# A perceiver kernel: keys of the second layer projected one block earlier, the maxima of a block dealt to other tiles, unread products in TensorE's waits, and the silu in two halves

## What is computed

```
def layer0(x):
    h = layernorm(x)
    q, k, v = h @ Wq.T + bq, ctx @ Wk.T + bk, ctx @ Wv.T + bv      # 16 heads of 16
    x = x + softmax(q @ k.T / 4 + (1 - mask) * -10000) @ v          # mask: 128 x 12544
    x = x + causal_linear_attention(layernorm(x))                   # then a gelu feed-forward
    h = layernorm(x)                                                # inputs and weights quantized
    return x + bitlinear(silu(bitlinear(h, w_gate)) * bitlinear(h, w_up), w_down)   # 256 -> 1024 -> 256

def layer1(x):                                                      # weights of its own, no mask
    x = x + (softmax(q @ k.T / 4) @ v) @ Wo.T + bo
    x = x + rwkv_time_mix(layernorm(x))
    return x + conv_ffn(layernorm(x))
```

## Time and profile before

| | |
|---|---|
| time of three runs | 1090.59, 1091.87, 1091.94 us; median 1091.87 |
| profiled execution | 1094.2 us, its span 1092.5 us, mean granted clock 0.975 |
| busy, us of the span | PE 1024.6, DVE 743.1, ACT 679.3, POOL 420.0 |
| L1091 of block 7's seven tiles and of block 8's first | 246.89, 251.47, 256.57, 261.14, 265.73, 270.32, 275.78, 280.63 us |
| durations at full clock elsewhere in the trace | a unit of keys (L1042) 1.67, the turns (L1119) 0.66, eight products such as L1312's (L1365) 1.05 us |
| scores of block 14's tiles 0 and 1 | start at 592.00 and 597.41 us, 5.41 apart |
| DVE's waits in the pair stage | 2.06 us ahead of 573.70, 1.76 ahead of 587.73 |
| first layer's blocks, last layer's | some 38 to 512 us, 592 to 1049 us |

### The profile page before, as it was taken

One profiled execution on the slowest core, in us unless ns is written; L12 is line 12 of the kernel. 1 busy time (PEld: TensorE's weight loads), 2 busy tenths in 40 slices (PEclk: granted clock), 3 DMA queues, 4 the chain that ended last, 5 costly groups with the idle time before them and its releaser, 6 DMA issues. The chain is left out here.

```text
span 1092.5 us, 30637 instructions
## 1 busy us (share of the span) xinstructions
PE 1024.6 (94%) x12851; PEld 687.2 (63%) x12851; DVE 743.1 (68%) x1714; ACT 679.3 (62%) x951; POOL 420.0 (38%) x374
## 2 busy tenths in 40 slices
PE   7899999999999999977878899999999999999877
PEld 4466666666666666655544576666666666666655
DVE  4788888888888888766347756655656555556555
ACT  3677777777778787765542555555655556555632
POOL 4268888888888888760100000000000000000000
PEclk9899999999999999998987999999999999999998
DMA  7410122201222012130031010111100111000000
GB/s 305 137 59 29 52 69 69 69 19 52 69 70 69 19 53 69 52 133 22 10 134 49 2 32 6 35 36 36 35 15 22 36 35 36 2 2 2 2 1 6
DMA packets 14682, 53.31 MB, mean 49 GB/s; under 512 B 3025, under 2 KB 4817, under 8 KB 13649
## 3 DMA queue, kind: packets, MB, share of 16 engines
q1 hardware_dynamic: 14544, 51.35, 13.6%
HBM read 51.21 MB, written 0.13 MB: 47 GB/s over the span
## 5 line engine op out<-in xcount | busy, mean ns | idle before, releaser
L740 DVE TENSOR_REDUCE tile_max<-ps_max 128x1 f32<-128x448 f32 x416 | 241.9, 620 | 161.1 <-PE ps_max L1054 159.7
L737 DVE CUSTOM_DVE_ANT_0 unread<-ps_max,masks 128x448 bf16<-128x448 f32 x432 | 253.5, 621 | 70.6 <-PE ps_max L1054 68.5
L413 POOL TENSOR_TENSOR probs<-probs,masks 128x512 f32<-128x512 f32 x182 | 227.8, 1273 | 77.9 <-ACT probs L526 76.9
L533 ACT ACTIVATE probs<-probs 128x1024 f32<-128x1024 f32 x196 | 207.4, 1058 | 58.7 <-DVE probs L795 46.7
L538 ACT ACTIVATE probs<-ps_scores 128x1024 f32<-128x1024 f32 x193 | 187.2, 1021 | 90.4 <-PE ps_scores L1095 90.3
L1095 PE MATMUL ps_scores<-q_pad,k_full 32*128 32x256 f32 x3088 | 233.9, 380 | 0.0
L1111 PE MATMUL ps_out<-probs,values 128*32 128x128 f32 x6272 | 214.9, 278 | 6.0 <-ACT probs L533 4.9
L1111 PEld LDWEIGHTS ps_out<-probs,values 128*32 128x32 f32 x6272 | 161.4, 111 | 58.8 <-issue 50.1
L1054 PE MATMUL ps_max<-k_high,q_high 32*128 32x448 bf16 x848 | 183.7, 360 | 14.0 <-DVE tile_max L740 7.6
L1095 PEld LDWEIGHTS ps_scores<-q_pad,k_full 32*128 32x128 f32 x3088 | 193.8, 188 | 1.0
L1042 PE MATMUL ps_proj<-ctx_t,wk 128*128 128x448 f32 x368 | 163.4, 567 | 0.0
(11 more groups left out here) (249 smaller groups left out, 787.7 us busy)
## 6 DMA issues: line engine op xcount, KB each, us to landing
ctx_t<-in_ctx_t SPq DMA_DIRECT2D x28, 896.0 KB, 5.3
masks<-in_mask_n SPq DMA_DIRECT2D x14, 448.0 KB, 3.4
masks<-in_mask_t SPq DMA_DIRECT2D x14, 448.0 KB, 3.6
room_w<-in_L_attn_f_w SPq DMA_DIRECT2D x2, 1024.0 KB, 8.9
room_w<-in_L_ffn_w SPq DMA_DIRECT2D x2, 1024.0 KB, 7.5
room_w<-in_L_ffn_w_gate SPq DMA_DIRECT2D x1, 1024.0 KB, 10.4
room_w<-in_L_ffn_w_up SPq DMA_DIRECT2D x1, 1024.0 KB, 12.9
room_w<-in_L_ffn_w_down SPq DMA_DIRECT2D x1, 1024.0 KB, 14.9
```

Source lines behind the costliest of these rows:

```text
L413: nc.gpsimd.tensor_tensor(p, p, three(mask_t[m % 2], TILES)[:, t, :].unsqueeze(1).to_broadcast([P, 4, P]), ALU.add).then_inc(sig("bias_add ...
L533: nc.scalar.activation(prob(T, half), prob(T, half), ACT.Exp).then_inc(sig(f"exp_done{half}"), 1)
L737: ins = v.tensor_tensor_reduce(unread[:, j % 2, :], max_bank(m, j)[:, 0:HALF], mask_n[m % 2][:, HALF * half:HALF * (half + 1)], 1.0, -3e38 ...
L740: ins = v.tensor_reduce(tile_max[:, h, half:half + 1], ps_max[:, j % 2, 0:HALF], AX_X, ALU.max)
```

## The change

1. `EXTRA_AT` of the first layer goes from (0, 2, 3, 4) to (1, 3, 5, 6); at 6 the extra is one of the block after next. The second layer keeps (0, 2, 3, 4). Block 0 has its own deal, and changes at tile 6 alone.
2. The keys of block 14 are projected in block 12, at tiles 0, 2, 4 and 6. `BETWEEN` has 14 units in another order, `BESIDE` two (behind pairs 1 and 4, both read by ACT at pair 5).
3. Unread products: `idents` (128 columns) at the very start and after the first turn, and in block 13, ahead of and behind the quantized stage's transposes, in the pair stage (one behind each pair from 6 to 15, four ahead of L1125) products of 256 columns.
4. The silu's table is loaded by a product of one column right after `ln_root(4)`; the silu and the multiply behind it go in two halves of 512 columns.

```diff
-        EXTRA_AT = (0, 2, 3, 4)
+        EXTRA_AT = ((1, 3, 5, 6), (0, 2, 3, 4))
...
+            one = int(t in EXTRA_AT[m // NB])
             if n + 1 < NB:
-                if t < LAST_AT:
-                    now = (2 if n == 0 else int(t in EXTRA_AT), 2, 2)
-                elif t == LAST_AT:
-                    now = (0, 2, 0)
+                if n == 0:
+                    now = (2, 2, 2) if t < LAST_AT else (0, 2, 0) if t == LAST_AT else now
+                elif t <= LAST_AT:
+                    now = (one, 2, 2 if t < LAST_AT else 0)
             if n + 2 < NB:
-                ahead = (0, 0, 2) if t == LAST_AT else (0, 2, 2) if t > LAST_AT else (0, 0, 0)
+                ahead = (0, 0, 2) if t == LAST_AT else (one, 2, 2) if t > LAST_AT else ahead
...
-        BETWEEN = [("k", NB, j) for j in range(4)] + [("k", NB + 1, j) for j in range(4)]
-        BETWEEN += [("v", NB, u) for u in range(PAIRS)] + [("k", NB + 2, j) for j in range(3)]
-        BESIDE = [("k", NB + 2, 3)] + [("v", NB + 1, u) for u in range(PAIRS)]
-        BESIDE_AT = (1, 4, 7, 10, 13)
+        BETWEEN = [("k", NB + 1, 0), ("k", NB + 1, 1), ("v", NB, 0), ("v", NB, 1), ("k", NB + 1, 2), ("v", NB, 2), ("k", NB + 1, 3),
+                   ("k", NB + 2, 0), ("v", NB, 3), ("v", NB + 1, 0), ("v", NB + 1, 1), ("v", NB + 1, 2)]
+        BETWEEN += [("k", NB + 2, 1), ("k", NB + 2, 2)]
+        BESIDE = [("k", NB + 2, 3), ("v", NB + 1, 3)]
+        BESIDE_AT = (1, 4)
         def keys_in_block(m):
-            return m < BLOCKS and m not in (NB, NB + 1, NB + 2)
+            return m < BLOCKS and m not in (NB + 1, NB + 2)
...
                     ln_root(4)
+                    act.wait_ge(sig("table_loaded"), 2)
+                    nc.scalar.activation(stat[:, 30:31], ones[:, 0:1], ACT.Silu).then_inc(sig("table_loaded"), 1)
                     between_out(8, 9)
...
-                    act.wait_ge(sig("gate_ready"), 1)
-                    nc.scalar.activation(gelu, ps_scores[:, 0:2, :].rearrange("p a n -> p (a n)"), ACT.Silu,
-                                         scale=stat[:, 20:21]).then_inc(sig("silu_ready"), 1)
+                    for half in range(2):
+                        act.wait_ge(sig("gate_ready"), half + 1)
+                        nc.scalar.activation(gelu[:, 512 * half:512 * (half + 1)], ps_scores[:, half, :], ACT.Silu,
+                                             scale=stat[:, 20:21]).then_inc(sig("silu_ready"), 1)
...
+                    for half in range(2):
+                        cols = slice(512 * half, 512 * (half + 1))
+                        dve.wait_ge(sig("gate_ready"), 3 + half)
+                        dve.wait_ge(sig("silu_ready"), 1 + half)
+                        note(v.scalar_tensor_tensor(out=big[:, cols], in0=ps_scores[:, 2 + half, :], scalar=stat[:, 21:22],
+                                                    in1=gelu[:, cols], op0=ALU.mult, op1=ALU.mult))
...
+            def idents(n):
+                for _ in range(n):
+                    mm(ps_out[:, 0:P], ident[:, :], ident[:, :], start=True, stop=True)
 
             pe.wait_ge(sig("idents"), 3)
+            idents(4)
...
                         if i in BESIDE_AT:
                             beside_in(BESIDE_AT.index(i))
-                    for u in range(len(BESIDE)):
-                        beside_read(u)
+                        elif i > 5:
+                            idle_products(1, ps_out)
+                        if i == 5:
+                            for u in range(len(BESIDE)):
+                                beside_read(u)
                 read_by[0] = ("max_copied", NB * l + 1)
+                idle_products(2 + 2 * l, ps_proj)
                 turn_max(NB * l)
...
                         projections(m, t)
+                        if m == NB - 1 and t > SUMS_AT:
+                            proj_free(None)
+                            idle_products(1, ps_proj)
...
+                if l == 0:
+                    idle_products(3, ps_proj)
                 weigh(NB * l + NB - 1, TILES - 1)
```

More of the change, by code:

```diff
@@ L562, in _ @@
                 if l == 1:
-                    between_out(14)
+                    between_out(13)
                 turned(4 * l, ps_max[:, 0, 0:D], xn_t[:, :, :].rearrange("p c t -> p (c t)"))
@@ L639, in _ @@
                     nc.scalar.copy(bigt.bitcast(BF16)[:, 0:D], ps_max[:, 0, :].bitcast(BF16)[:, 0:D]).then_inc(sig("xq_ready"), 1)
-                    act.wait_ge(sig("gate_ready"), 1)
-                    nc.scalar.activation(gelu, ps_scores[:, 0:2, :].rearrange("p a n -> p (a n)"), ACT.Silu,
-                                         scale=stat[:, 20:21]).then_inc(sig("silu_ready"), 1)
-                    between_out(10, 11, 12, 13)
+                    for half in range(2):
+                        act.wait_ge(sig("gate_ready"), half + 1)
+                        nc.scalar.activation(gelu[:, 512 * half:512 * (half + 1)], ps_scores[:, half, :], ACT.Silu,
+                                             scale=stat[:, 20:21]).then_inc(sig("silu_ready"), 1)
+                    between_out(10, 11, 12)
                     act.wait_ge(sig("hq_turned"), 1)
@@ L912, in _ @@
                     out_(quant(xn[:, :], D, bigq.bitcast(BF16)[:, 0:D], (0, 1), 20), "xq_made")
-                    dve.wait_ge(sig("gate_ready"), 1)
-                    dve.wait_ge(sig("silu_ready"), 1)
-                    link(v.scalar_tensor_tensor(out=big, in0=ps_scores[:, 2:4, :].rearrange("p a n -> p (a n)"), scalar=stat[:, 21:22],
-                                                in1=gelu, op0=ALU.mult, op1=ALU.mult))
+                    for half in range(2):
[4 more added lines that the diff above has]
+                                                    in1=gelu[:, cols], op0=ALU.mult, op1=ALU.mult))
+                    dve.wait_ge(sig("dve_link"), links[0])
                     out_(quant(big, FF, bigq.bitcast(BF16), (2,), 22), "hq_made")
@@ L1175, in between_in, with idle_products @@
                     (keys_in if what == "k" else values_in)(m, j, between_bank(u))
-            def idle_products(n):
+            def idle_products(n, bank=ps_out):
                 for _ in range(n):
-                    mm(ps_out[:, 0:D], ident[:, :], wq[0][:, 0, :], start=True, stop=True)
+                    mm(bank[:, 0:D], ident[:, :], wq[0][:, 0, :], start=True, stop=True)
+            def idents(n):
+                for _ in range(n):
+                    mm(ps_out[:, 0:P], ident[:, :], ident[:, :], start=True, stop=True)
             pe.wait_ge(sig("idents"), 3)
+            idents(4)
             for l in range(2):
@@ L1185, in _ @@
                 turn(xn, ps_max[:, 0, :]).then_inc(sig("turned"), 1)
+                if l == 0:
+                    idents(1)
                 pe.wait_ge(sig(f"q_weights{l}"), 32)
@@ L1192, in _ @@
                 if l == 1:
-                    between_read(14)
+                    between_read(13)
                 for zz in range(2):
@@ L1303, in _ @@
                                           tern[n][:, FF * k + 512 * half:FF * k + 512 * (half + 1)], start=(k == 0), stop=(k == DC - 1))
-                    last.then_inc(sig("gate_ready"), 1)
-                    between_in(10, 11, 12, 13)
+                            last.then_inc(sig("gate_ready"), 1)
+                    between_in(10, 11, 12)
+                    idle_products(1, ps_proj)
                     pe.wait_ge(sig("hq_made"), 1)
@@ L1309, in _ @@
                     last.then_inc(sig("hq_turned"), 1)
+                    idle_products(2, ps_proj)
                     pe.wait_ge(sig("hq_ready"), 1)
@@ L1314, in _ @@
                     last.then_inc(sig("down_ready"), 1)
-                    between_in(14)
+                    between_in(13)
             idle_products(3)
```

## The result

The changed kernel takes 1103.79 us (median of 8 runs, 1097.85 to 1107.55), the kernel before 1092.47 (8 runs, 1090.59 to 1094.66): a ratio of 1.0101, 95% interval 1.0082 to 1.0121. It is 11 us slower, where 1091.3 and a chance of 0.31 for slower had been forecast. The profiled execution of after took 1104.66, its span is 1102.9. In all that follows, executions that were slowed as a whole (one each of f, i, j and q, in each the profiled one) are left out.

What follows compares the result with a forecast made beforehand. PE's program with short waits bounds steady blocks; elsewhere a PE, ACT and DVE chain and the lower clock do. Terms: 9.6 - 2.8 + 0.2 - 3.2 - 1.8 - 1.4 - 1.2 = -0.6, from 1091.87 to 1091.3; range 1085 to 1097.

Steps and rivals of the forecast that it cites:

- Part 1: First layer's extras moved to tiles 1, 3, 5, 6: +0.82 a steady block, +9.6 us in all.
- the prediction's upper bound: For the moved extras in blocks 1 to 11: +14 (11 x 1.27), if no key tile gains.
- Part 2: Block 14's keys projected in block 12 fill PE's waits behind the maxima: -2.8; tile 6's unit costs nothing.
- Part 3: Block 13, products behind each weigh: ring lengthened by 1.2, clock staying up saves 1.0; +0.2.
- Part 4: Between the layers: silu halves -1.6, last product at full clock -0.8, order of units -0.8; -3.2.
- Parts 5 and 6: Pair stage: one of DVE's two waits goes, -1.8. Block 14: one of two slow first tiles won back, -1.4.
- Part 7: Start: unread products bring full rate sooner, 0.7 from the first keys and 0.5 from small steps; -1.2.
- (b): First layer's extras cost nothing, biases of tiles 5 and 6 still starting on time: about 1077; chance 0.15.
- (d): Pair stage: unread products keep PE behind DVE, ten pairs of 0.6 more, +6: about 1097; chance 0.16.
- (c): Unread products keep the clock wherever they stand, blocks 14 and 0 starting at full clock: about 1087; chance 0.22.
- (e): No clock is won in block 13, between the layers, block 14 or the start: about 1095.7; chance 0.13.

Runs made afterwards that it cites:

- f: Run a's kernel without the fourteen unread products of the pair stage: 1085.80 us, ratio 0.9928 to the kernel before.
- i: Kernel before with only block 14's keys in block 12 and the new lists of units between and beside: 1088.61 us, ratio 0.9972.
- j: Run g's kernel with five more unread products around block 14's tiles 0 and 1: 1076.43 us, ratio 0.9885 to the kernel before.
- q: Run l's kernel with eight more unread products ahead of the turn of block 0's maximum: 1086.14 us, ratio 0.9938 to the kernel before.
- a: Changed kernel with the first layer's extras back at tiles 0, 2, 3, 4: 1088.24 us, ratio 0.9948 to the kernel before.
- c: Changed kernel with DVE adding the last block's sums ahead of tile 1's bias, blocks 1 to 12: 1094.13 us, ratio 1.0009 to the kernel before.
- b: Kernel before with only the first layer's extras moved to tiles 1, 3, 5, 6: 1104.01 us, ratio 1.0107.
- d: Kernel before with only the unread products of the start: 1090.07 us, ratio 0.9975.
- h: Kernel before with only the silu and the multiply in halves and the table loaded early: 1089.03 us, ratio 0.9968.
- l: Run c's kernel (sums added first) with the first layer's extras at tiles 1, 2, 3, 4: 1079.76 us, ratio 0.9887 to the kernel before.
- g: Run a's kernel with four more unread products in the waits of the second layer's queries: 1083.76 us, ratio 0.9914 to the kernel before.
- m: Run l's kernel with the nine unread products of g and j: 1078.85 us, ratio 0.9874 to the kernel before.
- n: Changed kernel with tile 6's extra maximum behind the keys' products instead of ahead of the bias: 1106.01 us, ratio 1.013 to the kernel before.
- p: Run l's kernel with four more unread products ahead of the turn of block 0's maximum: 1083.51 us, ratio 0.9904 to the kernel before.

## Why the prediction was wrong

The forecast was 12.5 too low, and the miss has two halves. The deal was to cost 9.6 and costs 15.6 (a against the changed kernel): 6.0 missed. Parts 2 to 7 were to give back 10.2 and give back some 3.5 (a against the kernel before): 6.7 missed, less if the interval of a is taken.

**Part 1, the step that failed: "its product takes PE 0.18, about half of it in a wait: +0.10".** Tile 1 was costed by the extra's product alone. I had written of tile 5 that the bias is later and asked who waits for it; of tile 1 I did not ask. There the sums (L786) stand behind the bias on DVE and the values behind the sums on PE. Before, the sums were over 0.30 ahead of the values; DVE now starts its first maximum of the tile 0.20 later and has one more (0.62) ahead of the bias, and 0.82 later they are not. Measured +0.57, so a steady block pays 1.27 and not 0.82, and blocks 1 to 12 5.6 more. Run c takes 0.46 of the 0.57 away by the order on DVE alone. The rest of part 1 held: tile 5 +0.75 (0.73), tile 6 +0.54 (0.54), tiles 0, 2 and 4 -0.20 each (-0.19). Tile 3 has its extra before and after the change, so its +0.01 is the price of nothing. That a block cost 1.27, the number of the prediction's upper bound, is chance: the bound had no tile 1 in it and let no key tile gain, and tile 1 lost 0.57 while the key tiles gained 0.60.

**Part 2** came near its number: block 12 is 2.1 shorter where 2.8 were forecast, with 0.47 lost at tile 1 and 0.33 at tile 6, which was held to be free. But the gain is not the time of the filled waits. Before, the three waits of 1.2 lie in tiles 0, 2 and 4, and these take 4.57 to 4.59, as in a steady block; long were tiles 1 and 5, 6.67 and 6.99 at the lower clock. Run b's block 12, without keys but at a clock of 1.00, takes 32.81, less than the 34.13 with them. What the keys seem to buy is the clock: none of the eight profiles with them has a low stretch in block 12, three of the four without them have one.

**Part 3** held. In all eight profiled kernels that have its products the last weigh takes 1.08 and the turns 0.66, in the four without them 1.60 to 1.94 and 1.08 to 1.09; from block 13's first scores to the end of the turns it is 29.58 for 29.63 (+0.2 forecast).

**Part 4** was right in the silu: the reduce starts 3.02 behind the gate's first matmul (561.48 - 558.46) where it was 4.52, and the two halves of the multiply take 1.41 in sum for 1.28, as its working had it. The last product takes 1.05, but it does so in b, d and h too, which have no unread products there: the 1.89 was that one execution's clock. The order of the units brought 0.1, not 0.8: from the end of the turns to the gate it is 34.54 for 34.64. Of 0.46 won by the first turn of x most is lost again at a multiply of DVE (L910), which takes 1.03 in every profile with the change and 0.42 in those without; why is not shown.

**Parts 5 and 6 are the other step that failed, and the sum itself was of the wrong kind.** "The first stays (its unit of keys stays), the second goes: -1.8" and "I take one of the two back: -1.4": I took each low stretch of one execution as the cost of a place, and crossed it off where products were put. The profiles show that the stretches lie elsewhere from one execution to the next. In after the pair stage lost 1.4 where 1.8 were to be won: DVE still waits twice, 2.77 and 2.10, as both units ran at the lower clock (3.36 and 3.78). Block 14's tile 0 was at full clock (3.96, before 5.41) and tiles 1 and 2 paid (6.39 and 5.47). With the same program of the pair stage its reduces take 21.64 from first to last in after, 19.11 in a and 17.15 in c and l. Filling one wait (g) did not end it in block 14; with the waits filled up to a place where PE is busy without a break (m) the one profile taken is free of it, and the times of j agree.

**Part 7** came to its number (-1.3 for -1.2) by other terms. The first keys take 1.74 and not 3.33, more than the 0.7 assumed, but they start 1.18 later (9.88 for 8.70). Block 0's own 2.3 in the profile of after had no part in the sum; it is the clock of that execution, since b has it without any product.

**The rivals.** (b), that the extras cost nothing, is refuted by run b. (d) named the pair stage as what would make it slower; it did cost there, but by its units at the lower clock, while behind pair 5 the pairs are 1.11 apart and not 1.65, and the +11 is not from it: with the pair products and the old deal the kernel is faster than before. (c) and (e) are tested by a, which lacks part 1's 9.6. (c) comes to 1087.3 - 9.6 = 1077.7 then; a's median is 1088.2, and one of its twelve runs reached 1078.23. (e), no clock is won, comes to 1086.1 and is the nearest, though the end of block 13 and the start did gain.

**Still open:** what decides which of its two or more times an execution takes. The programs of after, n, a, c and l agree from block 13 on; their profiled executions take 105.4, 105.5, 102.0, 100.6 and 99.2 from there to block 14, a spread wider than the 4.8 that the parts were to win there. The time of arrival may matter; p and q don't separate it from what else they change.

## What to carry to other kernels

An instruction that is put ahead of another on its engine is to be costed at each place by all who wait for what now comes later, through the engine's order as well, and anew for each tile: the same extra cost 0.2 in tiles 0, 2 and 4, 0.54 in tile 6, 0.57 in tile 1 and 0.75 in tile 5, by who stood behind it, and 0.1 in tile 1 once the sums were added first. Do not price a low stretch of TensorE's clock by the place where one profile shows it: one profile shows one of several patterns, and a gain is to be judged by many runs and by other kernels with the same program in that stage. What came nearest to removing the stretches here was to fill every wait up to the stretch that is dense by itself (m, j).

## What the runs showed that was not expected

Two kernels that differ by 1.1 us in the sum of their tiles, a and l, differ by 8.5 in their medians (1088.24 and 1079.76), at mean clocks of about 0.98 and 0.99. Block 0 takes 35.63 to 35.64 (36.17 to 36.18 with tile 6's extra) in after, b, c, g and p, and 37.04 to 39.54 in before, a, d, h, l and m, at a clock of 1.00 in the first group and of 0.50 in part of tiles 0 and 1 in the second; neither the products at the start nor the deal sorts the two.
